# VectorE's attention loop written out; output bias added by TensorE, gating reads the projection from PSUM

## What is computed

```
ada = t_emb @ w_ada + b_ada
sh_msa, sc_msa, g_msa, sh_mlp, sc_mlp, g_mlp = split(ada, 6)
xn = layer_norm(logmap0(x))
xm = expmap0(xn * (1 + sc_msa) + sh_msa)
q, k, v = heads(plin(xm, w_q, b_q)), heads(plin(xm, w_k, b_k)), heads(plin(xm, w_v, b_v))
attn = softmax(einsum(log q, log k) / 4)
out_h = expmap0(einsum(attn, log v))
attn_out = plin(from_heads(out_h), w_o, b_o)       # plin(x, w, b) = expmap0(logmap0(x) @ w + b)
attn_t = g_msa * logmap0(attn_out)
x = mobius_add(residual, expmap0(attn_t))
... then the MLP half in the same manner, and x + result
```

## Time and profile before

| | |
|---|---|
| median of 3 runs | 818.61 us (817.21 to 820.23) |
| profiled execution | 816.74 us, its span 815.0 us |
| granted TensorE clock, mean over the span | 0.94 |
| busy share: PE, DVE, ACT, POOL | 80%, 82%, 65%, 41% |
| attention stage (from the first z to the last, on DVE) | 85.87 to 533.19 us |

### The profile page before, as it was taken

How to read it: one execution, slowest core, us unless ns; L and a number is a source line. 1 busy time by engine, 2 the same in 40 slices (tenths; PEclk the granted TensorE clock), 3 DMA queues, 4 the chain that set the end, 5 groups by cost and what they waited for, 6 DMA issues and landing times.

```text
span 815.0 us, 27718 instructions
## 1 busy us (share of the span) xinstructions
PE 655.6 (80%) x8355; PEld 468.1 (57%) x8369; DVE 671.9 (82%) x2230; ACT 531.5 (65%) x1563; POOL 337.5 (41%) x682
## 2 busy tenths in 40 slices
PE   5966988888888888888888887714669889989996
PEld 2655766666666666666666665502326556556654
DVE  2868898888889888888888898486997888888885
ACT  1125666667766666776666776334777888878884
POOL 1004555555555555555555555211233233134231
PEclk9979999999999999999999999555999999999999
DMA  9933755565555555565555654322443455445533
GB/s 322 357 98 89 137 130 119 131 134 124 134 129 129 123 129 134 123 133 118 129 128 125 133 132 98 76 65 65 117 117 102 125 150 155 131 130 155 152 96 104
DMA packets 184931, 107.53 MB, mean 132 GB/s; under 512 B 140202, under 2 KB 167730, under 8 KB 184883
## 3 DMA queue, kind: packets, MB, share of 16 engines
q1 hardware_dynamic: 183090, 104.11, 51.7%
q10 hardware_dynamic: 1792, 2.89, 1.0%
HBM read 64.24 MB, written 9.18 MB: 90 GB/s over the span
## 4 chain that ended last, share of the span: by engine, by line
DVE 34%; issue 29%; PE 15%; DMA 8%; DVEq 5%; ACT 4%; SPq 3%; POOL 2%; POOLq 0%; ACTq 0%
DVE hs L1151 7%; DVE lnx L1078 4%; PE p_s L948 3%; DVE g_all L1180 3%; DVEq L50 3%; SPq L365 3%; DMA mod_b<-mod_rows 2%; DMA qkT<-mod_b 2%; PE p_oz L859 2%; DMA x_all<-in_x 2%; PE p_qkv L948 2%; DVE fac L1200 2%; PE p_qkv L886 2%; DVE junk L1187 1%; PE p_t L934 1%
## 5 line engine op out<-in xcount | busy, mean ns | idle before, releaser
L886 PE MATMUL p_qkv<-wqkv,tT 128*128 128x256 f32 x768 | 197.2, 395 | 5.6 <-DVE u L1145 5.6
L886 PEld LDWEIGHTS p_qkv<-wqkv,tT 128*128 128x128 f32 x768 | 139.6, 195 | 22.8 <-issue 6.5
L859 PE MATMUL p_oz<-wo,oT 128*128 128x256 f32 x256 | 79.9, 439 | 6.0 <-ACT oT L624 0.5
L900 PEld LDWEIGHTS p_o<-v,pT 64*64 64x64 f32 x4096 | 67.9, 139 | 22.6 <-issue 22.6
L853 PE MATMUL p_oz<-ident,o 128*128 128x128 f32 x128 | 27.7, 300 | 63.4 <-DVE o L1165 55.1
L900 PE MATMUL p_o<-v,pT 64*64 64x17 f32 x4096 | 74.2, 211 | 0.0
L624 ACT ACTIVATE oT<-p_oz 128x256 f32<-128x256 f32 x64 | 24.6, 384 | 70.9 <-PE p_oz L853 70.9
L666 ACT ACTIVATE pT<-p_s 128x1024 f32<-128x1024 f32 x64 | 65.5, 1024 | 2.4 <-PE p_s L876 1.4
L1145 DVE SCALAR_TENSOR_TENSOR u<-p_qkv,ct,bqkv 128x768 f32<-128x768 f32 x64 | 64.4, 1006 | 3.2 <-PE p_qkv L886 3.2
L511 POOL TENSOR_TENSOR rt<-ss,c_mhalf 128x2 f32<-128x2 f32 x32 | 24.3, 760 | 101.7 <-ACT wqkv L714 99.0
L853 PEld LDWEIGHTS p_oz<-ident,o 128*128 128x128 f32 x128 | 13.3, 145 | 85.9 <-issue 80.7
(11 more groups left out here) (268 smaller groups left out, 1674.8 us busy)
## 6 DMA issues: line engine op xcount, KB each, us to landing
mod<-mod_rows SPq DMA_DIRECT2D x128, 128.0 KB, 2.8
x_all<-in_x SPq DMA_DIRECT2D x8, 1024.0 KB, 13.9
gate<-mod_rows SPq DMA_DIRECT2D x128, 64.0 KB, 2.8
mod<-mod_rows SPq DMA_DIRECT2D x32, 256.0 KB, 3.9
mod_b<-mod_rows SPq DMA_DIRECT2D x32, 256.0 KB, 4.0
out<-x_all SPq DMA_DIRECT2D x32, 256.0 KB, 2.2
gate<-gate_rows SPq DMA_DIRECT2D x32, 128.0 KB, 3.3
bqkv<-gate_rows SPq DMA_DIRECT2D x32, 128.0 KB, 3.8
```

Source lines behind the costliest of these rows:

```text
L859: mm = pe.matmul(p_oz[:, 0:D], oT[:, c, :, :].rearrange("p b s -> p (b s)"), wo[:, c, :], start=c == 0, stop=c == C - 1)
L886: mm = pe.matmul(p_qkv[:, a * D:a * D + D], tT[:, k, c, :], wqkv[:, c, a * D:a * D + D], start=c == 0, stop=c == C - 1)
L900: mm = pe.matmul(p_o[S * e:S * e + S, col:col + VW], pT[keys, e, g, :], v[keys, k, 2 * g + e, :], start=True, stop=True, skip_group_check= ...
```

## The change

Four edits, all in the attention stage:

1. VectorE's slots are written out from 0 to 70 (a Python loop, no hardware loop). The other engines keep theirs.
2. `add_bo` is gone. The output bias becomes a matmul at the head of `project_o`: a matrix of ones times `bo3`, whose first three rows hold b_o split into three bf16 parts (`split_bo`, once, in VectorE's slot 3), the rest zeros. `project_o` now writes `p_oz[:, D:2D]`, beside the transposes.
3. `gate_z` reads `p_oz[:, D:2D]` directly, and is now the last operation of VectorE's slot, for the tile in step L; `dot_x` stays a slot later. `square_z` reads `p_oz` too, behind `zg_ready`. TensorE's `output_waits` wait for both. The gate rows are fetched one slot sooner.
4. In VectorE's slot `modulate` moves from behind `scale_qk` to between `limit` and `factors`.

```diff
             def output_waits(i):
                 pe.wait_ge(o_ready, i + 1)
-                after(pe, z_ready, i)
+                after(pe, z_squared, i)
+                after(pe, zg_ready, i)
...
             def project_o(i):
                 pe.wait_ge(oT_ready, i + 1)
+                pe.wait_ge(bo3_ready, 1)
+                pe.matmul(p_oz[:, D:2 * D], ones16[:, :], bo3[:, :], start=True, stop=False)
                 for c in range(C):
-                    mm = pe.matmul(p_oz[:, 0:D], oT[:, c, :, :].rearrange("p b s -> p (b s)"), wo[:, c, :], start=c == 0, stop=c == C - 1)
+                    mm = pe.matmul(p_oz[:, D:2 * D], oT[:, c, :, :].rearrange("p b s -> p (b s)"), wo[:, c, :], start=False, stop=c == C - 1)
...
             def square_z(i, k):
-                act.wait_ge(z_ready, i + 1)
+                act.wait_ge(zg_ready, i + 1)
...
-                act.activation(junk[:, 1, :], z[:, :], ACT.Square, accum_out=st[:, k, 0:1]).then_inc(z_squared, 1)
+                act.activation(junk[:, 1, :], p_oz[:, D:2 * D], ACT.Square, accum_out=st[:, k, 0:1]).then_inc(z_squared, 1)
...
-            def add_bo(i):
+            def split_bo():
+                dve.wait_ge(bias_cleared, 3)
+                dve.tensor_scalar(not_first[:, 0:1], ident[:, 0:1], 1.0, None, ALU.subtract).then_inc(bo_part, 1)
+                dve.wait_ge(bo_part, 1)
+                dve.tensor_tensor(not_first[:, 1:2], not_first[:, 0:1], ident[:, 1:2], ALU.add).then_inc(bo_part, 1)
+                dve.wait_ge(bo_part, 2)
+                for n in range(2):
+                    dve.tensor_copy(bo3[0:3, :], bo_left).then_inc(bo_part, 1)
+                    dve.wait_ge(bo_part, 2 * n + 3)
+                    dve.scalar_tensor_tensor(out=bo_left, in0=bo3[0:3, :], scalar=not_first[0:3, n:n + 1], in1=bo_left,
+                                             op0=ALU.mult, op1=ALU.add).then_inc(bo_part, 1)
+                    dve.wait_ge(bo_part, 2 * n + 4)
+                dve.tensor_copy(bo3[0:3, :], bo_left).then_inc(bo3_ready, 1)
+
+            def gate_z(i, k, half):
                 dve.wait_ge(z_psum, i + 1)
-                after(dve, z_squared, i)
-                after(dve, zg_ready, i)
-                dve.tensor_tensor(z[:, :], p_oz[:, 0:D], bo[:, :], ALU.add).then_inc(z_ready, 1)
-
-            def gate_z(i, k, half):
-
-                dve.wait_ge(z_ready, i + 1)
                 dve.wait_ge(gate_in[k], 32 * half + 32)
...
-                dve.scalar_tensor_tensor(out=tile_of(g_all, i), in0=z[:, :], scalar=1.0, in1=gate[:, k, :],
+                dve.scalar_tensor_tensor(out=tile_of(g_all, i), in0=p_oz[:, D:2 * D], scalar=1.0, in1=gate[:, k, :],
...
                 if on(h, off, L_C):
                     project(2 * h + off - L_C, (off - L_C) % 2)
                 if on(h, off, L_G):
-                    gate_z(2 * h + off - L_G, (off - L_G) % 2, h + (off - L_G) // 2)
                     dot_x(2 * h + off - L_G, (off - L_G) % 2)
+                if s == 3:
+                    split_bo()
                 if isinstance(h, int) and 2 * h + off == T + L_L - 1:
                     split_ff_bias()
                 if on(h, off, L_L):
-                    add_bo(2 * h + off - L_L)
-
-            run_slots_rotated(dve, slot_until_rows, slot_from_sums, FIRST, T, T + L_G)
+                    gate_z(2 * h + off - L_L, (off - L_L) % 2, h + (off - L_L) // 2)
+
+            for s in range(T + L_G):
+                slot(s // 2, s % 2)
```

More of the change, by code:

```diff
@@ L112, in build @@
         bqkv = sb("bqkv", [P, 3 * D])
-        bo = sb("bo", [P, D])
+        bo3 = sb("bo3", [P, D], BF16)
+        bo_left = g_all[0:3, T - 5, :]
         b2 = sb("b2", [P, D])
@@ L238, in build @@
         oT_psum = sem("oT_psum"); oT_ready = sem("oT_ready")
-        z_psum = sem("z_psum"); z_ready = sem("z_ready"); zg_ready = sem("zg_ready")
+        z_psum = sem("z_psum"); zg_ready = sem("zg_ready")
         xg_summed = sem("xg_summed"); z_squared = sem("z_squared"); zg_squared = sem("zg_squared")
@@ L246, in build @@
         gate2_in = [sem(f"gate2_in{k}") for k in range(2)]
-        bias_cleared = sem("bias_cleared"); bias_part = sem("bias_part")
+        bias_cleared = sem("bias_cleared"); bo_part = sem("bo_part"); bo3_ready = sem("bo3_ready"); bias_part = sem("bias_part")
         xa_ready = sem("xa_ready"); x1_ready = sem("x1_ready"); ln2_half = sem("ln2_half")
@@ L303, in run_slots @@
                 slot(s // 2, s % 2)
[L305 to L319, removed]
         def count(n):
@@ L388, in slot @@
                                  qk4s[k].rearrange("p a h r d -> p (a h r d)"), transpose=True).then_inc(qkT_in, 16)
-                if on(h, off, L_L):
-                    i, k = 2 * h + off - L_L, (off - L_L) % 2
+                if on(h, off, L_H):
+                    i, k = 2 * h + off - L_H, (off - L_H) % 2
                     after(sp, zg_ready, i - 1)
@@ L443, in _ @@
             pool.memset(ones16[:, :], 1.0).then_inc(bias_cleared, 1)
+            pool.memset(bo3[:, :], 0.0).then_inc(bias_cleared, 1)
             pool.wait_ge(consts_made, 1)
@@ L1111, in split_ff_bias @@
                 dve.wait_ge(ffw_made, 8)
[L1112 to L1116, removed]
                 for n in range(2):
                     dve.tensor_copy(bias, left).then_inc(bias_part, 1)
-                    dve.wait_ge(bias_part, 2 * n + 3)
+                    dve.wait_ge(bias_part, 2 * n + 1)
                     dve.scalar_tensor_tensor(out=left, in0=bias, scalar=not_first[0:3, n:n + 1], in1=left,
                                              op0=ALU.mult, op1=ALU.add).then_inc(bias_part, 1)
-                    dve.wait_ge(bias_part, 2 * n + 4)
+                    dve.wait_ge(bias_part, 2 * n + 2)
                 dve.tensor_copy(bias, left).then_inc(ff_bias_made, 1)
@@ L1221, in repeat_parts, with slot @@
                 dve.tensor_copy(k4[:, :, 1, :, :], k4[:, :, 0, :, :]).then_inc(again_ready, 1)
-            def slot_until_rows(h, off):
+            def slot(h, off):
                 if on(h, off, L_E):
                     limit(2 * h + off - L_E)
+                if on(h, off, L_A) and not at_start(h, off):
+                    modulate(2 * h + off - L_A, (off - L_A) % 2, h + (off - L_A) // 2)
+                if on(h, off, L_E):
                     factors(2 * h + off - L_E)
                     scale_qk(2 * h + off - L_E, (off - L_E) % 2)
-                if on(h, off, L_A) and not at_start(h, off):
-                    modulate(2 * h + off - L_A, (off - L_A) % 2, h + (off - L_A) // 2)
                 if on(h, off, L_A):
```

3 lines of the change are left out of this document (1 added, 2 removed).

## The result

| | before | after |
|---|---|---|
| median of 4 runs | 819.42 us (817.21 to 821.41) | 784.13 us (780.54 to 785.67) |
| ratio, 95% interval | | 0.9564 (0.9522 to 0.9606) |
| span of the profiled execution | 815.0 us | 782.0 us |
| first z of the stage, last z (gating in its place) | 85.87, 533.19 us | 87.86, 497.76 us |
| the 57 slots from the first z on | 405.95 us, 7.12 each | 369.51 us, 6.48 each |

A forecast was written before the change was run, and what follows sets the result against it. Bound: a per-slot cycle through DVE and PE, 6.56 us after the change. Span 815.0 - 32.0 + 1.1 + 0.9 + 2.0 = 787.0, plus 1.7 around it, scaled by 1.0023: 790 us, range 780 to 806.

The forecast's parts named there:

- The bound: Attention loop: neither DVE nor PE alone sets the pace, but a cycle running through both in each slot.
- the first step, writing out: VectorE's attention slots: without the hardware loop each takes 6.45 us, as in the written-out slots, against 7.12 on average.
- The ring: Attention slot: DVE from z to `o` (4.16 us), PE through the projection (2.29), then z again; 6.56 after the change.
- Gating in the addition's place, +0.11: Start of DVE's slot: `gate_z` holds DVE 0.45 us where the z addition held it 0.34, so +0.11 us a slot.
- Bias matmul, +0.15: PE, ahead of the projection: the added matmul lengthens each slot by 0.15 us, bounds 0.11 and 0.30.
- `modulate` moved, -0.15: DVE between `rlim` and t: lnx fills waiting gaps, saving 0.15 us a slot, bounds -0.23 and 0.
- PSUM read, 0: DVE's gating: reading PSUM instead of SBUF adds nothing; rival of dearer reads, 794 us, chance 5%.
- DVE's room beside PE: DVE between `o` and the gating: it would wait about 0.5 us a slot for PE's projection.
- that very chain: From `rlim` through `scale_qk`, ACT's copy and POOL's `scale_v` to the roots: 6.22 us, hidden under 6.56.
- Instruction fetch, 0: DVE's written-out program: fetching costs nothing; rival of stalls, 3.3 us per fetch, 833 us, chance 4%.
- The rival's sign: DVE's profile: gaps put down to issue at intervals of some slots would show the prediction wrong.
- the slow-clock slot that I kept (1.1): Attention loop: of four slots lengthened by a falling granted clock, one would remain, costing 1.1 us.

The follow-up runs named there:

- e1: The kernel before with only VectorE's slots written out, nothing else changed: 782.28 us, ratio 0.9572 to the kernel before.
- e8: The changed kernel without the bias matmul, b_o left out of the computation: 781.91 us, ratio 0.9579 to the kernel before.
- e11: e9 without the bias matmul, b_o left out of the computation: 771.75 us, ratio 0.9409 to the kernel before.
- e9: e5 with `modulate` for the next tile run between `dot_x` and `gate_z`, mod rows fetched a slot sooner: 772.06 us, ratio 0.9422 to the kernel before.
- e5: The changed kernel with the next tile's mod rows issued ahead of the gate rows in SyncE's queue: 772.02 us, ratio 0.9457 to the kernel before.
- e6: The changed kernel with 22 one-element memsets at the head of VectorE's program, shifting later instructions: 782.55 us, ratio 0.9576 to the kernel before.
- e4: The changed kernel with `modulate` put back behind `scale_qk`: 788.09 us, ratio 0.9638 to the kernel before.
- e12: e5 with the two f16 copies (`repeat_parts`) behind `project` instead of ahead of it: 789.64 us, ratio 0.9646 to the kernel before.

## Why the prediction was right, and where its steps were wrong

**The bound and the first step, writing out: right.** The two written-out slots in the trace of before foretold e1: 6.45 against 6.46 to 6.47 measured over the whole stage.

**The ring: right in form, too long in size.** It gave 6.45 + 0.11 + 0.15 - 0.15 = 6.56 us; the short slots are 6.25 to 6.28, with the ring as their bound. Term by term in the slot above:

- *Gating in the addition's place, +0.11: wrong, 0.01.* `rlim` starts 0.35 after the gating (386.27 to 386.62), where 0.34 stood. The 0.45 that I took was the start of `dot_x`, which needs `g_all` and so waits for it; `rlim` needs nothing of it. A start-to-start time includes the follower's dependency, and I moved it to a follower that has none.
- *Bias matmul, +0.15: 0.02*, since the projection behind it became 0.10 shorter. e8 and e11 leave nothing to be seen.
- *`modulate` moved, -0.15: -0.24.* `rlim` to t is 388.00 - 386.62 = 1.38 instead of 1.62; all gaps were filled. My own working had given 1.39 to 1.44, and I had taken less than it.
- *PSUM read, 0: right.* Gating has 0.425 us over all 64 against 0.409 for `dot_x`'s like instruction from SBUF. The 62 cycles of the Trainium skill ("VectorE: DVE Perf Modes", the TRN2 errata) would be 0.065; the trace shows 0.016.

The measured ring of that slot is 3.93 us from gating to the end of `o` (4.16 + 0.01 - 0.24) and 2.35 on to the next gating (2.29 + 0.02, and 0.04 more ahead of the transposes), 6.28. In the shortest slots the 0.04 is missing: 6.45 + 0.01 + 0.02 - 0.24 = 6.24, as measured.

**Missed: DVE's room beside PE.** The forecast had DVE wait about 0.5 us for the projection in each slot; it has 0.06 to 0.13 of room. From e1's queue (6.47 less 0.10 of room) DVE's slot lost 0.34 (z), 0.12 (the gap behind `g_all`) and 0.24 (the move), and gained 0.50 between `o` and `u` (0.87 to 1.37): 6.17. The 0.50 is the copy: `scale_qk` is later by the length of lnx, so POOL's subtraction and `scale_v` are too, the copies wait for the first and run beside the second. The prediction had looked at that very chain and asked only if it was longer than the ring (6.22 against 6.56), not what it would run beside. In the changed kernel the 0.50 cost nothing yet, since the ring is longer still; with it in the queue the shorter ring of e9 gained nothing.

**Missed: the mod rows.** The step "`modulate` moved" costed the work that moves, and not the DMA that must be there for it. Price, by e5: 8.7 us of the slots. The ratios say the same, 0.9564 to 0.9457 or 8.8 us; the medians (784.13 to 772.02, each beside other runs of the kernel before) say 12.

**Instruction fetch, 0: wrong by little.** The rival's sign, gaps put down to issue at intervals of some slots, was there. The forecast had named it as a sign of being wrong, and on this step it was wrong; e6 moved the gap with the instructions. Its size was 0.32 us a slot (6.25 to 6.57), 14 times, 4.5 us, not 3.3 each. The page prints 0.23 because it counts from the shown end of `hs`: from start to start, `hs` to `rden` is 383.24 - 382.81 = 0.43 with the gap and 389.50 - 389.38 = 0.12 without, and this 0.31 is on the ring. The Trainium skill ("Runtime: NRT & Kernel Launch") calls it mostly hidden; the trace agrees, 4.5 of 370 us are left.

**The sum.** 57 x 6.25 = 356.3, + 4.5 fetch, + 8.7 mod rows, makes 369.5. (The 8.7 is the difference to e5, so only the first two terms, 360.8, are tested, by e5's slots.) I had 373.9 + 1.1: the ring was 17.6 too dear, the two missed waits 13.2 too cheap, and the slow-clock slot that I kept (1.1) did not occur (granted clock 1.00 from 100 to 440 us, 0.98 before). Outside the 57 slots the first z is 2.0 later (forecast 2.0, `split_bo`; in part luck, since with the same `split_bo` it is 0.7 later in e5 and 3.6 later in e4), the last six take 40.4 instead of 41.4 (forecast +0.9), and from the last z to the end of the span 284.2 instead of 281.8 (forecast 0); the other kernels have 280.5 to 284.2 there, with a program that is the same in all, so I put that to scatter. In sum -33.0 for the span where -28.0 was forecast. The direction did not hang on errors cancelling, the closeness did: part of it is luck. And the gain as a whole is that of edit 1. What edits 2 to 4 took off the ring (6.47 to 6.25) went to the mod rows and the fetch gaps, so that e1 is as fast.

**Still open.** That the gaps are fetching is argued from their place and their spacing; no row shows a fetch landing at one. Nor was it tried to give `u` a third buffer, which should give e12 its short copies without the wait.

The best versions are e5 and e9, 0.946 and 0.942 of the kernel before, 1 to 1.5% under the changed kernel. Their intervals overlap, so they are not ranked.

## What to carry to other kernels

When a trace holds the same work in and out of a loop, that pair of rows is worth more than any costing: it gave this forecast. An edit's worth depends on which bound it meets: the same two edits cost 6 us in one order of VectorE's queue and gained 23 in another. A page that prints no wait doesn't say which bound holds; the distance from the end of the work waited for to the start of the waiter does, 0.04 us in every slot here against 0.3 and more where VectorE's queue was the bound. When a step moves ahead, list three things that move with it: its inputs' DMAs and what they queue behind, the followers on other engines, and what those then run beside.

## What the runs showed of the hardware

- **A VectorE f16 copy that starts while a GpSimd tensor operation runs ends 0.15 us after it.** 0.28 us alone, 0.64 beside `scale_v`: 205.19 + 0.64 against 205.06 + 0.62 in e9, 390.96 against 390.81 in the changed kernel. Operations of 51 columns do the same on their scale. In the kernel before a copy starts 0.07 into one and takes 0.36 (below); in e12 the first copy starts 0.13 into one and takes 0.29. A GpSimd operation that starts after the copy does not lengthen it. The Trainium skill ("GPSIMD Engine Reference", Specifications) tells of contention of GpSimd with VectorE's instructions in a two-port mode or with two SBUF inputs; the trace agrees, though no row shows in which mode the copy ran.

```profile
175.96 0.36 DVE L1221 COPY mod_b<-mod_b 128x512 f16<-128x512 f16 x1
...
175.89 0.28 POOL L459 TENSOR_TENSOR nw<-y 128x51 f32<-128x51 f32 x1
```

- **Written-out code on VectorE shows a short gap each 128 instructions.** The gap is 0.15 to 0.25 us, at a fixed place in the program (e6), with 11 packets more on the instruction queue. On the ring it costs 0.32 us (e5). In e9 `rden` has the same gap and the slot grows by 0.02 to 0.05 only, since `o` to `u` then takes 1.08 us instead of 1.38: the copies come late enough for POOL.
- **A register-driven loop costs more than its branch.** 7.08 us a slot against 6.47 for the same instructions written out: one gap of 0.4 at the branch each second slot, and gaps such as the 0.20 ahead of `fac` in each.
- **A matmul ahead of a chain can hide its first weight load.** Four fp32 matmuls took 1.13 us (before, and e8), and 1.03 behind a bf16 one that itself added 0.12; their weight loads start at 391.36, beside the bf16 matmul and 0.12 ahead of the first of them.
